# Expert steps of a mixture-of-experts block: activations laid out as 128 and twice 48 rows, five down products, transposes ahead of the down products

## The chip, the cores and the metric

The kernel runs on one NeuronCore of a Trainium2 chip. The metric is the time of one launch in device microseconds (us). The engines are PE (TensorE; PEld are its weight loads), DVE (VectorE), ACT (ScalarE), POOL (GpSimd) and SP (SyncE); each works through its own list of instructions in order and waits on semaphores.

## What is computed

One transformer block on 2048 rows of 256 numbers: a windowed attention, then a router that picks 4 of 16 experts for each row, the experts, and one shared expert for all rows. The change lies in the experts alone:

```python
w, idx = _router(xf, rg_w, ru_w, extra_scale, extra_bias)      # top 4 of 16
coeff = jnp.einsum('tk,tke->te', w, one_hot(idx, 16))
def step(y, ew):
    wg, wu, wd, c = ew                                         # 176x256, 176x256, 256x176
    h = jax.nn.silu(xf @ wg.T) * (xf @ wu.T)                   # 176 activations a row
    return (y + h @ wd.T * c[:, None], None)
y, _ = lax.scan(step, zeros, (Wg, Wu, Wd, coeff.T))
z = jax.nn.silu(xf @ Sg.T) * (xf @ Su.T) @ Sd.T                # the shared expert, 352 activations
x = x + gb * (y + z)
```

## The kernel before

Every fp32 product is made of three products of a reduced type: both factors are split into a high part (a copy to that type) and a low part (what is left), and high x high, low x high and high x low are summed in PSUM (`three`, L101).

The rows are sorted by expert through a scratch in HBM. Then come `NS` = 79 **expert steps** of 128 rows each (numbered 0 to 78), every one with the expert that a table names, so that the weights are addressed through a register; after them 16 **shared steps** (n = 0 to 15) of 128 rows for the shared expert. Both are software-pipelined over four lists. In step s:

- PE: `gate_up(s)`, six products into `GU`; `transpose_x(s+2)`, two transposes into `XT`; `down(s-2)`, six products into `YP`; `transpose_a(s-1)`, two transposes of the activations into `HT`. The 176 activations are taken as two blocks of 88 rows (`FH` = 88), so that down has two blocks of three products.
- ACT: `gate(s)` (silu), `x_hi(s+2)`, `a_hi(s-1)` (the high part of the transposed activations), and two small copies (`pick`).
- DVE: `gating(s)` (the activations `h_act`), `x_lo(s+2)`, `y_gate(s-2)` (the result times its coefficient), `a_lo(s-1)` (the low part). Eleven of steps 0 to 13 also carry `gu_low`, the low part of one expert's gate and up weights (704 columns); the last four steps carry four such pieces for the shared expert.
- POOL: it scatters the results of s to HBM by an indirect DMA, and in steps 0 to 7 makes `dn_low`, the low part of one expert's down weights. SP loads the 128 rows of step s+4.

The semaphores that matter: `down(w)` waits for `aT_lo` of w, `transpose_a(w)` for `gated` of w, `gate_up(w)` for `xT_lo2` of w, `y_gate(w)` for `y_mm` of w. `h_act`, `HT`, `aT`, `XT`, `GU` and `YP` have two buffers each. A shared step has twelve gate and up products, three transposes of 128 columns and nine down products; `add_late(n)` on DVE adds its result to the output.

## Time and profile before

| what | value |
|---|---|
| time, median of 3 runs | 569.58 us (567.87 to 569.83) |
| the profiled execution: its span, first to last instruction | 566.3 us |
| expert steps: first products of step 0 to those of shared step 0 | 321.2 to 502.2 us of the span |
| one expert step, steps 18 to 74 | 2.21 us |
| PE busy over the span | 87% |

The span is what the trace shows; a run's time has some 3.3 us more around it (569.58 less 566.3). Time stamps below are from the span's start. A group of instructions that overlap in their pipeline has a longer busy time than the distance between their starts, so that the distance is what counts for an engine that is full.

### The profile page before, as it was taken

Reading aid. Unit: us, or ns where it says so; the run is one execution under the profiler, and the core shown is the slowest. Engines: PE = TensorE matmul, PEld = TensorE weight load, DVE = VectorE, ACT = ScalarE, POOL = GpSimd, SP = SyncE. Lnnn points to the kernel's source line nnn. Section 1 sums busy time; section 2 is a strip of 40 time slices with the busy share of each in tenths; the row PEclk is TensorE's granted clock in tenths of the full one; section 3 lists DMA queues with packets and bytes.
Section 4 is the critical chain, followed back from the end, with each engine's and each line's share of the span. In section 5 each row is a group of like instructions: output and inputs, shape, how many; then the busy total and the mean of one; then the engine's idle time right before and its main releaser. Section 6 shows DMA issues by size and latency. Waiting matters only on the chain. (4 is left out here: it accounts for less than half of the span.)

```text
span 566.3 us, 12354 instructions
## 1 busy us (share of the span) xinstructions
PE 492.5 (87%) x3575; PEld 464.1 (82%) x3575; DVE 396.3 (70%) x1099; ACT 284.1 (50%) x743; POOL 291.9 (52%) x330
## 2 busy tenths in 40 slices
PE   2699999999999999998430488999999999999996
PEld 0589998999999898988330377999999999999995
DVE  6769953456867768687763798867777776784575
ACT  2368754554554545533262564555655655553331
POOL 6446603010346446465766799544444444446994
PEclk9999999999999999999555599999999999999999
DMA  7457996779747456422858443343434444356951
GB/s 196 134 170 217 254 307 205 196 206 229 209 125 216 139 164 183 124 86 83 267 203 271 135 132 103 116 136 119 140 120 127 132 124 137 119 158 249 413 204 74
DMA packets 62982, 98.00 MB, mean 173 GB/s; under 512 B 9747, under 2 KB 48210, under 8 KB 61574
## 3 DMA queue, kind: packets, MB, share of 16 engines
q1 hardware_dynamic: 50664, 57.80, 37.8%
q0 software_dynamic: 9136, 32.53, 15.2%
q10 hardware_dynamic: 3118, 6.89, 3.9%
q8 instruction: 31, 0.51, 0.4%
q14 instruction: 33, 0.27, 0.2%
HBM read 60.49 MB, written 40.04 MB: 178 GB/s over the span
## 5 line engine op out<-in xcount | busy, mean ns | idle before, releaser
L1702 POOL DMA_INDIRECT ys_scr<-h,ids_st x59 | 61.0, 1033 | 67.4 <-DVE h L1756 63.9
L140 POOL DMA_INDIRECT xs_scr<-h,slot_u x64 | 62.9, 982 | 54.0 <-PE TB L1302 26.6
L105 PE MATMUL GU<-gu_hi,xT 128*128 x316 | 84.1, 348 | 1.9 <-DVE xT L1736 1.9
L1626 ACT ACTIVATE aT<-HT 88x256 fp32r<-88x256 f32 (+1 forms) x95 | 37.8, 399 | 65.9 <-PE HT L1862 65.9
L105 PE MATMUL YP<-dn_hi,aT 88*128 x316 | 67.1, 304 | 4.4 <-DVE aT L1741 3.9
L1748 DVE TENSOR_TENSOR h_act<-GU,g_act 128x176 f32<-128x176 f32 (+1 forms) x95 | 35.2, 371 | 46.4 <-ACT g_act L1619 46.2
L919 ACT ACTIVATE prob<-TB 128x512 f32<-128x512 f32 x64 | 38.2, 597 | 56.5 <-PE TB L1302 55.8
L1312 PE MATMUL O<-raw,prob 128*128 128x99 f32 x512 | 66.2, 275 | 0.0
L1312 PEld LDWEIGHTS O<-raw,prob 128*128 128x128 f32 x512 | 61.6, 192 | 0.1
L105 PEld LDWEIGHTS YP<-dn_hi,aT 88*128 88x128 f32 x316 | 47.5, 188 | 11.1 <-issue 7.5
L105 PEld LDWEIGHTS GU<-gu_hi,xT 128*128 128x128 f32 x316 | 52.1, 192 | 2.3 <-issue 2.3
L1619 ACT ACTIVATE g_act<-GU 128x176 f32<-128x176 f32 (+1 forms) x95 | 32.4, 341 | 42.2 <-PE GU L105 42.0
L1741 DVE TENSOR_TENSOR aT<-HT,aT 88x256 fp32r<-88x256 f32 (+1 forms) x95 | 42.0, 442 | 15.4 <-ACT aT L1626 5.8
L105 PE MATMUL GU<-lo,xT 128*128 x158 | 51.7, 327 | 0.0
L1852 PE MATMUL XT<-ident,x_st 128*128 128x128 f32 x190 | 37.2, 278 | 15.3 <-DMA x_st<-xs_scr 15.2
L1044 DVE TENSOR_REDUCE neg_m<-SB 128x4 f32<-128x512 f32 x64 | 41.8, 686 | 6.4 <-PE SB L1290 6.0
L105 PE MATMUL YP<-lo,aT 88*128 x158 | 44.2, 280 | 0.0
L1852 PEld LDWEIGHTS XT<-ident,x_st 128*128 128x128 f32 x190 | 26.7, 143 | 18.8 <-DMA x_st<-xs_scr 16.1
L1736 DVE TENSOR_TENSOR xT<-XT,xT 128x256 fp32r<-128x256 f32 x95 | 39.9, 421 | 0.4 <-ACT xT L1613 0.3
L1290 PEld LDWEIGHTS SB<-dn_hi,gu_hi 97*128 97x128 f32 x240 | 36.2, 191 | 2.7
L1302 PEld LDWEIGHTS TB<-gu_hi,dn_hi 97*128 97x128 f32 x240 | 36.2, 191 | 2.7
L1862 PE MATMUL HT<-ident,h_act 128*88 128x128 f32 (+1 forms) x206 | 37.9, 272 | 0.0
(243 smaller groups left out, 1252.8 us busy)
## 6 DMA issues: line engine op xcount, KB each, us to landing
x_st<-xs_scr SPq DMA_DIRECT2D x79, 144.0 KB
dn_hi<-k_scr SPq DMA_DIRECT2D x48, 192.0 KB, 3.8
planes<-ys_scr POOLq DMA_DIRECT2D x8, 1024.0 KB, 17.1
k_scr<-raw SPq DMA_DIRECT2D x8, 768.0 KB, 6.1
dn_hi<-q_scr SPq DMA_DIRECT2D x24, 256.0 KB, 4.4
q_scr<-raw SPq DMA_DIRECT2D x8, 512.0 KB, 3.6
raw<-in_egu SPq DMA_DIRECT2D x8, 352.0 KB
raw<-in_x SPq DMA_DIRECT2D x16, 128.0 KB, 4.0
```

Source lines behind the costliest of these rows:

```text
L105: mm = eng.matmul(out, a, b, start=(i + j == 0), stop=(i == len(pairs) - 1 and j == 2))
L140: eng.indirect_dma_start(T["xs_scr"], bass.IndirectOffsetOnAxis(ap=T["slot_u"][:, par, t % 2, k:k + 1], axis=0), T["h2"][:, row, :], None) ...
L919: eng.activation(prob[:, q, :], TB[q % 2][:, :], ACT.Exp, scale=SCALE).then_inc(exp_done, 1)
L1044: eng.tensor_reduce(neg_m[:, p2, 4 * q:4 * q + 4], SB[q % 2][:, :].rearrange("p (h x) -> p h x", h=4), AX.X, ALU.max, negate=True).then_in ...
L1290: mm = eng.matmul(bank[:, hh * P:(hh + 1) * P], queries(n, t, 4 * q + hh), keys(par, 4 * q + hh, j), start=False, stop=True, skip_group_ch ...
L1312: mm = eng.matmul(O[:, head // 8, at:at + WIDE * VC], prob[:, q, hh * P:(hh + 1) * P], VW[:, bass.ds(HEADS * n + head, WIDE), :].rearrange ...
L1626: eng.activation(aT[0:rows, p2, 0, 0:k, :], HT[p2][0:rows, 0:k * P].rearrange("p (k x) -> p k x", k=k), ACT.Copy).then_inc(aT_hi, 1)
L1702: eng.indirect_dma_start(ys, bass.IndirectOffsetOnAxis(ap=ids_st[:, r:r + 1].bitcast(U32), axis=0), results(r % 8), None).then_inc(sent[q] ...
L1736: eng.tensor_tensor(xT[:, p2, 1, :, :], XT[p2][:, 0:D].rearrange("p (k x) -> p k x", k=KD), xT[:, p2, 0, :, :].bitcast(F32), ALU.subtract) ...
L1741: eng.tensor_tensor(aT[0:rows, p2, 1, 0:k, :], HT[p2][0:rows, 0:k * P].rearrange("p (k x) -> p k x", k=k), aT[0:rows, p2, 0, 0:k, :].bitca ...
L1852: mm = eng.transpose(XT[t % 2][:, k * P:(k + 1) * P], x_st[:, t, k * P:(k + 1) * P], ident[:, :])
L1862: mm = eng.transpose(HT[p2][0:rows, k * P:(k + 1) * P], h_act[:, p2, k * rows:(k + 1) * rows], ident[:, :])
```

## The change

The 176 activations are no longer cut in the middle. The first 128 make one block. The other 48 (`REST`) stand twice in the second block, at rows 0 to 47 and 64 to 111 (`SLOT` = 64), the rows between being zero: DVE writes them twice (one multiplication of 48 columns more), and after the transposes takes the high part off the second copy in place, so that one operand holds the high part above and the low part below. The second block of the down weights holds its 48 rows twice in the same places (the host lays them out so, with zeros between), and the block then needs two products (with the weights' high and low part) in place of three. `down` has five products. The low part of the activations is made by two instructions (64 rows x 128, 128 rows x 128) in place of one (88 rows x 256). Loads, high parts and low parts of the down weights have 128 rows in place of 88, and the memset of `h_act` 416 columns in place of 64.

The order moves too: on PE `transpose_a(s-1)` stands ahead of `down(s-2)`, on DVE `a_lo(s-1)` ahead of `y_gate(s-2)`, in the shared steps likewise, and after the last step the last but one down products stand ahead of the last transposes.

```diff
@@ gating, a_lo and step on DVE @@
+            if width == FI:
+                eng.tensor_tensor(h_act[:, p2, P + SLOT:P + SLOT + REST], up[:, P:FI], g_act[:, p2, P:FI], ALU.mult)
             eng.tensor_tensor(h_act[:, p2, 0:width], up, g_act[:, p2, 0:width], ALU.mult).then_inc(gated, 1)
-            eng.tensor_tensor(aT[0:rows, p2, 1, 0:k, :], HT[p2][0:rows, 0:k * P].rearrange("p (k x) -> p k x", k=k),
-                              aT[0:rows, p2, 0, 0:k, :].bitcast(F32), ALU.subtract).then_inc(aT_lo, 1)
+            eng.tensor_tensor(aT[SLOT:P, p2, 0, 1, :], HT[p2][SLOT:P, P:2 * P], aT[SLOT:P, p2, 0, 1, :].bitcast(F32),
+                              ALU.subtract)
+            eng.tensor_tensor(aT[:, p2, 1, 0, :], HT[p2][:, 0:P], aT[:, p2, 0, 0, :].bitcast(F32), ALU.subtract).then_inc(aT_lo, 1)
...
             x_lo(s + 2, p2)
+            if runs(s, 1):
+                a_lo(s - 1, 1 - p2)
             if runs(s, 2):
                 y_gate(s - 2, (r - 2) % UNROLL, i if r % 4 >= 2 else i - 1)
-            if runs(s, 1):
-                a_lo(s - 1, 1 - p2, FH, 2)
@@ down and step on PE @@
-            three(eng, YP[p2][:, 0:D],
-                  [(aT[0:FH, p2, 0, k, :], aT[0:FH, p2, 1, k, :], dn_of(dn_hi, e, k), dn_of(lo, e, k))
-                   for k in range(2)]).then_inc(y_mm, 1)
+            high, low, rest = aT[:, p2, 0, 0, :], aT[:, p2, 1, 0, :], aT[:, p2, 0, 1, :]
+            pairs = ((rest, dn_of(dn_hi, e, 1)), (rest, dn_of(lo, e, 1)), (high, dn_of(dn_hi, e, 0)),
+                     (low, dn_of(dn_hi, e, 0)), (high, dn_of(lo, e, 0)))
+            for i, (a, b) in enumerate(pairs):
+                mm = eng.matmul(YP[p2][:, 0:D], a, b, start=(i == 0), stop=(i == len(pairs) - 1))
+            mm.then_inc(y_mm, 1)
...
+            if runs(s, 1):
+                transpose_a(w - 1, 1 - p2)
             if isinstance(s, int) and 2 <= s < NE + 2:
                 eng.wait_ge(dn_lo, s - 1)
             if runs(s, 2):
                 down(w - 2, p2, before)
-            if runs(s, 1):
-                transpose_a(w - 1, 1 - p2, FH, 2)
@@ after the last shared step on PE @@
-        transpose_a(NS + TILES - 1, p2, P, SH_K)
-        for w in (NS + TILES - 2, NS + TILES - 1):
-            shared_down(w, w % 2)
+        shared_down(NS + TILES - 2, 1 - p2)
+        transpose_shared(NS + TILES - 1, p2)
+        shared_down(NS + TILES - 1, p2)
```

PE's list in an expert step before, from the load of the expert's number on (ISA sets up the register for the weights' address; the digit after `XT`, `YP`, `HT`, `GU` is the buffer):

```order
582 L1529 TENSOR_LOAD step_i
583 L1852 MATMUL XT0<-ident,x_st 128x128 x2
584 L105 ISA
585 L105 MATMUL YP0<-dn_hi,aT 128x256 x2
586 L105 ISA
587 L105 MATMUL YP0<-lo,aT 128x256
588 L105 ISA
589 L105 MATMUL YP0<-dn_hi,aT 128x256 x2
590 L105 ISA
591 L105 MATMUL YP0<-lo,aT 128x256
592 L1862 MATMUL HT1<-ident,h_act 88x128 x2
593 L105 ISA
```

The same place now:

```order
567 L1529 TENSOR_LOAD step_i
568 L1861 MATMUL XT1<-ident,x_st 128x128 x2
569 L1871 MATMUL HT0<-ident,h_act 128x128
570 L1872 MATMUL HT0<-ident,h_act 128x128
571 L1911 ISA
572 L1911 MATMUL YP1<-dn_hi,aT 128x256
573 L1911 ISA
574 L1911 MATMUL YP1<-lo,aT 128x256
575 L1911 ISA
576 L1911 MATMUL YP1<-dn_hi,aT 128x256 x2
577 L1911 ISA
578 L1911 MATMUL YP1<-lo,aT 128x256
```

The two transposes of the activations have moved from behind the down products to ahead of them, and of six down products five are left.

DVE's list in one of the first expert steps before, a step with a `gu_low` (the row `lo<-raw,gu_hi`); `h2<-YP` is a `y_gate`:

```order
639 L1748 TENSOR_TENSOR h_act<-GU1,g_act 128x176
640 L1736 TENSOR_TENSOR xT<-XT1,xT 128x256
641 L1756 SCALAR_TENSOR_TENSOR h2<-YP1,coef,gb 128x256
642 L1741 TENSOR_TENSOR aT<-HT0,aT 88x256
643 L1788 TENSOR_TENSOR lo<-raw,gu_hi 128x704
```

The same place now:

```order
648 L1756 TENSOR_TENSOR h_act<-GU1,g_act 128x48
649 L1757 TENSOR_TENSOR h_act<-GU1,g_act 128x176
650 L1736 TENSOR_TENSOR xT<-XT1,xT 128x256
651 L1742 TENSOR_TENSOR aT<-HT0,aT 64x128
652 L1744 TENSOR_TENSOR aT<-HT0,aT 128x128
653 L1765 SCALAR_TENSOR_TENSOR h2<-YP1,coef,gb 128x256
654 L1797 TENSOR_TENSOR lo<-raw,gu_hi 128x704
```

Two instructions came to DVE's step, and the low part of the activations moved ahead of the result.

## Rows read from the trace of the kernel before

**Rows 1.** Chain that ended last, steps 36 and 37: start us, us, engine, tile, line, count.

```profile
402.05 0.79 PE YP L105 x6
402.84 0.22 PE HT L1862 x2
403.06 0.97 PE GU L105 x6
404.03 0.22 PE XT L1852 x2
```

**Rows 2.** Busy time by stretch; PEclk is the granted clock.

```profile
326.00:358.00 32.00, 27.64 (x189) 24.85 (x188) 28.84 (x58) 17.60 (x65) 28.80 (x22) 1.00 0.40 113
...
367.50:493.30 125.80, 125.69 (x914) 120.61 (x913) 89.50 (x229) 74.02 (x285) 54.78 (x58) 1.00 0.41 128
493.30:502.20 8.90, 8.90 (x67) 8.52 (x65) 8.12 (x20) 6.58 (x21) 4.47 (x5) 1.00 0.37 120
```

**Rows 3.** Timeline of ACT in the same steps: start, us, [idle before <-releaser].

```profile
403.10 0.38 ACT L1626 ACTIVATE aT<-HT 88x256 fp32r<-88x256 f32 x1 [0.63 <-PE HT L1862]
```

**Rows 4.** Timeline of DVE in the same steps.

```profile
402.21 0.34 DVE L1748 TENSOR_TENSOR h_act<-GU,g_act 128x176 f32<-128x176 f32 x1 [0.48 <-ACT g_act L1619]
...
403.51 0.42 DVE L1741 TENSOR_TENSOR aT<-HT,aT 88x256 fp32r<-88x256 f32 x1
```

**Rows 5.** Timeline of PE in the same steps.

```profile
404.07 0.49 PE L105 MATMUL YP<-dn_hi,aT 88*128 x2
```

**Rows 6.** The chain again: the first shared step and a later one.

```profile
504.61 0.69 PE YP L105 x6
...
511.34 1.03 PE YP L105 x9
512.37 0.33 PE HT L1862 x3
```

**Rows 7.** Timeline of PE where steps 14, 18 and 75 begin.

```profile
358.29 0.57 PE L105 MATMUL GU<-gu_hi,xT 128*128 x2
...
367.58 0.56 PE L105 MATMUL GU<-gu_hi,xT 128*128 x2
...
493.35 0.57 PE L105 MATMUL GU<-gu_hi,xT 128*128 x2
```

**Rows 8.** Timeline of DVE in the first expert steps.

```profile
338.18 1.69 DVE L1788 TENSOR_TENSOR lo<-raw,gu_hi 128x704 fp32r<-128x704 f32 x1
339.79 0.33 DVE L1748 TENSOR_TENSOR h_act<-GU,g_act 128x176 f32<-128x176 f32 x1
340.04 0.41 DVE L1736 TENSOR_TENSOR xT<-XT,xT 128x256 fp32r<-128x256 f32 x1
340.37 0.47 DVE L1756 SCALAR_TENSOR_TENSOR h<-YP,coef,gb 128x256 f32<-128x256 f32 x1
340.76 0.41 DVE L1741 TENSOR_TENSOR aT<-HT,aT 88x256 fp32r<-88x256 f32 x1
341.10 0.32 DVE L1748 TENSOR_TENSOR h_act<-GU,g_act 128x176 f32<-128x176 f32 x1
...
342.43 0.48 DVE L1756 SCALAR_TENSOR_TENSOR h<-YP,coef,gb 128x256 f32<-128x256 f32 x1 [0.67 <-PE YP L105]
```

**Rows 9.** Groups of instructions by form: count | busy us, mean ns.

```profile
L1681 POOL TENSOR_TENSOR lo<-raw,dn_hi 88x512 fp32r<-88x512 f32 x16 | 23.7, 1495 | 6.5 <-POOLq L1992 6.3
...
L1729 POOL TENSOR_TENSOR planes<-planes 128x512 f32<-128x512 f32 x12 | 15.5, 1293 | 1.8 <-DMA to_add<-x_scr 1.8
```

**Rows 10.** The chain at the end of the program.

```profile
558.07 0.50 ACT aT L1626
...
559.21 1.30 PE YP L105 x9
...
560.88 0.56 DVE aT L1741
...
561.48 1.34 PE YP L105 x9
```

More of the change, by code:

```diff
@@ L20 @@
 NE, TOPK, FI = 16, 4, 176
-FH = FI // 2
+REST, SLOT = FI - P, P // 2
 SH_I = 2 * FI
@@ L174, in split_hi @@
     eng.activation(T["gu_hi"][:, e, :], T["raw"][:, e, 0:W_GU], ACT.Copy).then_inc(T["w_hi2"], 1)
-    eng.activation(T["dn_hi"][0:FH, e, :], T["raw"][0:FH, e, W_GU:W_EXP], ACT.Copy).then_inc(T["w_hi2"], 1)
+    eng.activation(T["dn_hi"][:, e, :], T["raw"][:, e, W_GU:W_EXP], ACT.Copy).then_inc(T["w_hi2"], 1)
 def fill_up(nc, eng, A, T, low, high):
@@ L1619, in gate, with a_hi @@
             eng.activation(g_act[:, p2, 0:width], bank[:, 0:width], ACT.Silu).then_inc(silu, 1)
-        def a_hi(w, p2, rows, k):
+        def a_hi(w, p2, k):
             eng.wait_ge(ht_mm, w + 1)
@@ L1625, in a_hi @@
                 eng.wait_ge(y_mm, w - 1)
-            eng.activation(aT[0:rows, p2, 0, 0:k, :], HT[p2][0:rows, 0:k * P].rearrange("p (k x) -> p k x", k=k),
+            eng.activation(aT[:, p2, 0, 0:k, :], HT[p2][:, 0:k * P].rearrange("p (k x) -> p k x", k=k),
                            ACT.Copy).then_inc(aT_hi, 1)
@@ L1671, in _ @@
             if n == 0:
-                a_hi(NS - 1, 1 - p2, FH, 2)
+                a_hi(NS - 1, 1 - p2, 2)
             else:
-                a_hi(NS + n - 1, 1 - p2, P, SH_K)
-        a_hi(NS + TILES - 1, (NS + TILES - 1) % 2, P, SH_K)
+                a_hi(NS + n - 1, 1 - p2, SH_K)
+        a_hi(NS + TILES - 1, (NS + TILES - 1) % 2, SH_K)
     @block.gpsimd
@@ L1788, in gu_low @@
             eng.tensor_tensor(lo[:, e, 0:W_GU], raw[:, e, 0:W_GU], gu_hi[:, e, :].bitcast(F32), ALU.subtract).then_inc(gu_lo, 1)
-        eng.memset(h_act[:, :, SH_I:SH_K * P], 0.0).then_inc(h_zero, 1)
+        eng.memset(h_act[:, :, FI:SH_K * P], 0.0).then_inc(h_zero, 1)
         for e in range(3):
@@ L1827, in _ @@
                 x_lo(NS + n + 2, p2)
+            if n == 0:
+                a_lo(NS - 1, 1 - p2)
+            else:
+                shared_lo(NS + n - 1, 1 - p2)
             if n < 2:
@@ L1834, in _ @@
                 add_late(n - 2)
-            if n == 0:
-                a_lo(NS - 1, 1 - p2, FH, 2)
-            else:
-                a_lo(NS + n - 1, 1 - p2, P, SH_K)
             for g in range(KEPT // 2):
@@ L1856, in x_pairs, with transpose_a, transpose_shared @@
             return xT[:, p2, 0, k, :], xT[:, p2, 1, k, :]
-        def transpose_a(w, p2, rows, blocks):
+        def transpose_a(w, p2):
             eng.wait_ge(gated, w + 1)
-            for k in range(blocks):
-                mm = eng.transpose(HT[p2][0:rows, k * P:(k + 1) * P], h_act[:, p2, k * rows:(k + 1) * rows], ident[:, :])
+            eng.transpose(HT[p2][:, 0:P], h_act[:, p2, 0:P], ident[:, :])
+            eng.transpose(HT[p2][:, P:2 * P], h_act[:, p2, P:2 * P], ident[:, :]).then_inc(ht_mm, 1)
+        def transpose_shared(w, p2):
+            eng.wait_ge(gated, w + 1)
+            for k in range(SH_K):
+                mm = eng.transpose(HT[p2][:, k * P:(k + 1) * P], h_act[:, p2, k * P:(k + 1) * P], ident[:, :])
             mm.then_inc(ht_mm, 1)
@@ L1929, in _ @@
                 transpose_x(w + 2, (w + 2) % 4, (w + 2) // 4 + 1)
+            if n == 0:
+                transpose_a(w - 1, 1 - p2)
+            else:
+                transpose_shared(w - 1, 1 - p2)
             if n < 2:
@@ L1933, in _ @@
                 shared_down(w - 2, p2)
-            if n == 0:
-                transpose_a(w - 1, 1 - p2, FH, 2)
-            else:
-                transpose_a(w - 1, 1 - p2, P, SH_K)
-        transpose_a(NS + TILES - 1, p2, P, SH_K)
-        for w in (NS + TILES - 2, NS + TILES - 1):
-            shared_down(w, w % 2)
+        shared_down(NS + TILES - 2, 1 - p2)
+        transpose_shared(NS + TILES - 1, p2)
+        shared_down(NS + TILES - 1, p2)
 def program(nc, A, out):
@@ L2057, in by_dim, with down_rows @@
         return np.asarray(w).reshape(2, HEADS // 2, DH, D).transpose(0, 2, 1, 3).reshape(D, D)
+    def down_rows(w):
+        rows = np.zeros((P, NE, 2, D), np.float32)
+        t = np.asarray(w).transpose(2, 0, 1)
+        rows[:, :, 0] = t[:P]
+        for first in (0, SLOT):
+            rows[first:first + REST, :, 1] = t[P:]
+        return rows
     g = {k.replace("L0_ffn_", "").replace("L0_attn_", "").replace("L0_", ""): np.asarray(v) for k, v in x.items()}
```

22 lines of the change are left out of this document (13 added, 9 removed).

## Prediction

> **What bounds the kernel now.** I read the chain that ended last first, for the expert steps hold 181 of the 566 us of the span. In a plain step (most of steps 14 to 74) it never leaves PE: six down products 0.79 us, two transposes of activations 0.22, six gate and up products 0.97, two transposes of rows 0.22, together 2.20 [rows 1]. The busy table by stretch says the same: over steps 18 to 74 PE is busy 125.69 of 125.80 us at the full granted clock, DVE 89.50 and POOL 54.78 [rows 2]. So a product taken off PE should show in the time. The second thing to see is that PE's "busy" hides a wait. Six expert down products take 0.79 us in a plain step, but 0.69 in the first shared step [rows 1, 6], where twelve gate and up products stand ahead of them and their operand is long ready. In the plain step the timelines show why: the transposes of the activations end at 403.06 [rows 1], ACT makes the high part from 403.10 to 403.48 [rows 3], DVE the low part from 403.51 to 403.93, and the first down product starts at 404.07 [rows 4, 5]. PE has finished the work in between by about then and waits some 0.10 us; the products in flight keep it counted as busy. That is a loop of four engines, and it sets the step, not PE's work alone.
>
> The opening is another regime. From 326 to 358 us, steps 2 to 13, DVE is busy 28.84 of 32.00 us and PE only 27.64 [rows 2]. The timeline shows DVE's rows without a gap, step after step, wherever a gu_low stands in them [rows 8].
>
> **The change part by part.**
>
> Sixth product. Nine shared down products, 128 rows deep, take 1.03 us, 0.114 each; the six of 88 rows took 0.69, 0.115 each [rows 6]. So the depth costs nothing, and one product less is 0.115 us a step.
>
> Transposes of 128 columns in place of 88: three take 0.33 in a shared step, two of 88 took 0.22 [rows 6, 1]: 0.11 each either way, nothing.
>
> The order on PE. Low parts of s-1 are now needed a whole step later, behind gate_up, four transposes and the down products of s-2. The 0.10 us goes. What is late next? transpose_a(s-1) now stands ahead of down(s-2), and its wait for gating holds those down products, and through them y_gate and POOL's scatter. In the trace gating runs from 402.21 to 402.55 [rows 4]; its gate and up products ended one step before those that end at 404.03 [rows 1], at 401.83, so it is done 0.72 us after them. With the new instruction ahead of it, that is some 0.85. The transposes want it 0.22 + 0.22 + 0.58 + 0.97 + 0.22 = 2.2 us after that point. Cover 1.35 us: nothing in a plain step.
>
> A plain step is then 0.97 + 0.22 + 0.22 + 5 x 0.115 = 1.98 us against 2.20, a gain of 0.22 (0.115 for the product, 0.105 for the wait). DVE must follow in 1.98. Its chain, from start to start where it is full, is 0.25 (h_act), 0.33 (xT), 0.39 (result), 0.34 (aT), 1.31 together [rows 8].
>
> What the change adds on DVE. From 176 to 256 columns the distance grows by 0.08, so 0.001 a column and 0.07 for an instruction: 48 columns take 0.12, and 128 columns 0.20, two of them 0.40 in place of 0.34. The low bound is 0.19 a step. The high bound takes every instruction's full busy time instead (0.33, 0.41 and so on [rows 8], less the columns): 0.20 + 2 x 0.28 - 0.34 = 0.42, and a little for the overlap that the neighbours lose: 0.45. No row that I read has a DVE instruction on rows 64 to 127 among others that begin at row 0, so neither end is shown. I take 0.32, the middle. The step's chain is then 1.63, at most 1.76, and ends inside 1.98: nothing in a plain step.
>
> One rule of the Trainium skill speaks to this (VectorE: DVE Perf Modes, section "Two Vector instructions with no wait between them"): a Vector instruction that begins in another group of 32 partitions than the one before it in the same memory is held until all earlier ones have finished. By it the piece on rows 64 to 127 and the one behind it both wait, the overlap of 0.08 is lost twice, the addition is 0.35, and the sum below would end at 557.8; without it, at the low bound, at 555.8. No row here shows it.
>
> The opening, steps 0 to 13. Twelve full steps at 0.32 on an engine without gaps are 3.8 us, steps 0 and 1 some 0.3, the wider memset, 352 columns more at 0.001, at most 0.35, taken as 0.3. Against it stand DVE's 3.16 us of idle time in that stretch [rows 2]: its gaps are waits for down products that wait for DVE, as the 0.67 ahead of the result at 342.43 [rows 8], a turn of the loop that the new order opens. I let 2.0 of it go; the rest waits for ACT's high parts of weights. Opening: +2.4 (from 12 x 0.19 + 0.5 - 3.0 = -0.2 to 12 x 0.45 + 0.7 - 1 = +5.1).
>
> Wider down weights. POOL's low parts are 512 columns of 88 rows, 1495 ns as a mean beside a busy DVE; its sums of 512 columns and 128 rows take 1293 [rows 9]. Rows cost nothing there, nor on ACT. The loads grow by 40 rows of 2 KB an expert, 1.3 MB in all, most of it before the experts begin; the DMA engines are busy 0.4 of the time in the expert steps [rows 2]. I count nothing.
>
> Steps 14 to 17 take 367.58 - 358.29 = 9.29 us [rows 7] and become 4 x 1.98 = 7.92: -1.4. Steps 18 to 74 are 57 in 493.35 - 367.58 = 125.77 [rows 7]: 57 x 0.22 = 12.5 off. In the last four, DVE is busy 8.12 of 8.90 us [rows 2] with the shared expert's low parts, and 4 x 0.32 is more than its 0.78 idle: DVE wants 9.4, PE may run the 1.35 us of cover ahead of it, and I count nothing (-0.9 to +0.5). The first two shared steps lose one product each, -0.2; the other shared steps hold no such wait and stay.
>
> The end. The last but one down products wait for their low part until 559.21 and run 1.30; the last low part cannot start before 560.88, behind the sum of those products on DVE; the last products run 1.34 from 561.48 [rows 10]. In the new order the last but one low part is made during the nine products ahead (1.03 [rows 6]), so these products start about 1.0 us sooner; behind them come the last transposes (0.33 [rows 6]), ACT (0.50) and DVE (0.56) [rows 10], with the hand-overs 1.5 in place of the 0.97 from 560.51 to 561.48: 0.5 back. Net -0.5.
>
> Sum: +2.4 - 1.4 - 12.5 + 0 - 0.2 - 0.5 = -12.2. The profiled span of 566.3 becomes 554.1; with the 3.3 us that lie around it, the median of 569.6 becomes **557.4**.
>
> **Rivals.**
>
> DVE sets the plain step. If nothing on it overlaps, its step is 0.20 + 0.34 + 0.42 + 0.28 + 0.28 + 0.48 = 2.0 to 2.05 us and the gain 0.16: 57 x 0.16 = 9.1, the opening +5.1, the end steps +0.5: 569.6 + 5.1 - 0.9 - 9.1 + 0.5 - 0.7 = 564.5. For it: the new instruction on rows 64 and up, unseen so far. Against it: its rows do overlap in every full stretch [rows 8].
>
> The 0.10 us stays, because it is PE's own cost of turning from transposes to products whose weights are addressed by register, not the wait. Then 61 steps gain 0.115: 557.4 + 6.4 = 563.8. Against it: the first shared step turns in the same way and shows 0.69 [rows 6].
>
> The change does not do what it says, since something else paces a step at 2.2 us (the setting of registers, the row loads, POOL): only the opening's cost is left, 569.6 + 2.4 - 0.7 = 571.3, no change. Against it: POOL and DMA have half of the step free [rows 2].
>
> Slower. DVE's chain becomes serial with PE's. The place is each plain step: if the idle 0.48 ahead of h_act [rows 4] stays in the chain, and every instruction counts in full, a step is 2.05 + 0.48 + 0.1 = 2.6, 0.42 over the present one: 57 x 0.42 = 24, the opening +5: about 598. It decides from 2.21 us a step on, 0.9 of added work. Against it: no wait of PE closes that loop, since h_act of step s is wanted only in step s+1.
>
> **How the numbers follow.** Forecast 0.71, DVE paces 0.12, the wait stays 0.08, nothing moves 0.05, slower 0.04. The forecast's own range goes from 554.5 (opening -0.2) to 561 (opening +5.1). Runs of this kernel differ by 0.35%, so that 0.5%, 2.8 us, is about what can be told from no change. All but the last two cases are faster by more; I leave 0.02 more for a mishap within the bound. Range 553.8 to 564.8: it takes in the first three cases and leaves some 0.13 out, theirs and the last two.
>
> **What would show it.** In the trace after: a plain step of 1.98 us from gate and up to gate and up; five down products in 0.58 of the chain; the low part ready more than a microsecond before them; DVE's chain at 1.5 to 1.75 where it is full, and whether the piece on rows 64 to 127 starts only when the one before it has ended; the opening to step 14 longer or shorter than now by at most 3 us. A plain step of 2.05 with DVE without gaps is the first rival, 0.69 for five products the second, 2.2 the third. I am wrong if the steps gain less than 0.15, or if the opening costs more than 5 us.

## The result and the profile after

The changed kernel takes 561.14 us (median of six runs, 559.41 to 562.00) against 569.21 of the kernel before in the same job: a ratio of 0.985, 95% interval 0.981 to 0.988. The forecast was 557.4, the range 553.8 to 564.8: the direction and the range were right, the size was 3.7 us too good. The profiled run took 562.0, with a span of 560.1 in place of 566.3. Ratios leave out the runs that fell in a slower state of the chip, among them one of the order alone (568.18).

The page after: the first line is busy time and share by engine, the second the shares of the chain that ended last.

```profile
PE 480.7 (86%) x3496; PEld 454.3 (81%) x3496; DVE 414.3 (74%) x1257; ACT 274.6 (49%) x743; POOL 288.1 (51%) x330
...
PE 26%; DVE 8%; DMA 5%; issue 2%; POOL 1%; ACT 1%; ACTq 0%; DVEq 0%; POOLq 0%
```

PE has 79 products less, one for each expert step. DVE has 158 instructions more, and it now has 8% of the chain, the DMA 5%.

The busy windows after, to be read beside [rows 2]: stretch and length, then PE, PEld, DVE, ACT, POOL, granted clock, DMA share, GB/s. They are steps 2 to 13, 14 to 17, 18 to 74 and 75 to 78.

```profile
328.10:362.10 34.00, 27.58 (x183) 24.36 (x181) 33.47 (x83) 17.60 (x70) 27.83 (x23) 1.00 0.36 113
362.10:370.70 8.60, 8.40 (x60) 8.07 (x61) 7.96 (x27) 4.31 (x18) 3.61 (x4) 1.00 0.47 128
370.70:485.10 114.40, 114.20 (x857) 112.06 (x856) 100.49 (x343) 67.78 (x286) 54.68 (x57) 1.00 0.47 141
485.10:494.80 9.70, 8.72 (x62) 7.98 (x61) 9.36 (x29) 6.42 (x22) 4.33 (x5) 1.00 0.45 142
```

Steps 18 to 74 fell from 125.8 to 114.4 us, PE still full. In steps 2 to 13 DVE is now busy 33.47 of 34.00, and in steps 75 to 78 9.36 of 9.70 while PE has a whole microsecond free: DVE sets the time there, though in steps 2 to 13 a part of its busy time is a wait for POOL, as the experiments show.

A plain step in the chain after (start us, us, engine, tile, line, count), beside [rows 1]:

```profile
402.04 0.22 PE XT L1861 x2
402.26 0.11 PE HT L1871
402.37 0.11 PE HT L1872
402.48 0.59 PE YP L1911 x5
403.07 0.96 PE GU L105 x6
404.04 0.22 PE XT L1861 x2
```

From transposes to transposes this is 2.00 us; the average of the undisturbed steps is 1.986, against 1.98 forecast and 2.20 before. DVE's low part and the down products that want it, from the timelines of the same steps:

```profile
403.55 0.29 DVE L1744 TENSOR_TENSOR aT<-HT,aT 128x128 fp32r<-128x128 f32 x1
404.23 0.36 PE L1911 MATMUL YP<-dn_hi,aT 128*128 x1
```

The low part is ready at 403.84, 0.39 us ahead of the products. The prediction looked for more than a microsecond there.

The next table has the durations of the stages in every kernel of this study, each the distance between two starts in PE's timeline: "first" is the start of the first expert product (in us of the span), "14-17" the time from the first product of step 14 to that of step 18 and so on; "shared 2-14" goes to the start of the last shared step, "end" from there to the end of the last sum on DVE, and "store" is what follows it in the span.

| kernel | first | 0-13 | 14-17 | 18-74 | 75-78 | shared 0-1 | shared 2-14 | end | store |
|---|---|---|---|---|---|---|---|---|---|
| before | 321.2 | 37.05 | 9.29 | 125.77 | 8.89 | 6.72 | 45.52 | 8.78 | 3.0 |
| after | 323.9 | 38.14 | 8.65 | 114.41 | 9.68 | 6.73 | 46.58 | 8.33 | 3.7 |
| after, again (e11) | 321.9 | 38.13 | 8.66 | 114.43 | 9.69 | 6.72 | 46.59 | 8.33 | 3.4 |
| order alone (e1) | 325.2 | 33.50 | 8.45 | 120.37 | 8.44 | 6.67 | 46.36 | 8.33 | 5.3 |
| five products alone (e2) | 320.7 | 38.25 | 10.01 | 131.52 | 9.95 | 6.73 | 45.83 | 8.78 | 2.4 |
| before, wide loads (e5) | 320.3 | 36.93 | 9.20 | 125.74 | 8.88 | 6.74 | 45.97 | 8.79 | 2.4 |
| no hold, by a mask (e3) | 322.2 | 36.31 | 8.43 | 113.88 | 9.16 | 6.74 | 46.58 | 8.34 | 3.7 |
| no hold, rows 0 to 63 (e9) | 322.8 | 36.06 | 8.36 | 113.67 | 8.97 | 6.74 | 46.83 | 8.33 | 3.4 |
| one low part (e7) | 322.6 | 36.05 | 8.28 | 113.83 | 8.83 | 6.74 | 46.67 | 8.34 | 3.4 |
| entries loaded once (e6) | 320.9 | 38.15 | 8.61 | 113.25 | 9.69 | 6.73 | 46.67 | 8.33 | 3.4 |
| sums a step later (e4) | 323.5 | 38.16 | 8.68 | 114.41 | 9.68 | 6.72 | 46.94 | 8.32 | 3.8 |
| e7 + e6 + e4 (e8) | 322.5 | 36.18 | 8.31 | 113.22 | 8.82 | 6.73 | 46.72 | 8.37 | 3.8 |
| e7 + e6, sums spread (e10) | 322.1 | 36.41 | 8.29 | 113.23 | 8.83 | 6.73 | 46.66 | 8.36 | 3.8 |
| e7 + e6, pair sooner (e12) | 321.5 | 36.03 | 8.27 | 113.25 | 8.83 | 6.73 | 45.64 | 8.33 | 5.1 |

The stages repeat within 0.05 us from one trace of the changed kernel to the next. The first and the last column don't: they hold the attention and the landing of the last store. So stages are compared with stages below, and whole times only with their scatter in mind. The ratios are each to the kernel before in the same job; between jobs that kernel's own median goes from 569.2 to 570.8.

### The profile page after: what moved, and what is told of

The parts are those of the page before. It is cut to its first block and busy times, and to the rows that moved or that the text cites. A ratio compares the mean times of both kernels' runs of the same rounds, so it can differ in the third digit from the quotient of the medians.

```text
span 560.1 us, 12354 instructions
## 1 busy us (share of the span) xinstructions
PE 480.7 (86%) x3496; PEld 454.3 (81%) x3496; DVE 414.3 (74%) x1257; ACT 274.6 (49%) x743; POOL 288.1 (51%) x330
## 5 line engine op out<-in xcount | busy, mean ns | idle before, releaser
L1702 POOL DMA_INDIRECT ys_scr<-h,ids_st x59 | 58.4, 990 | 63.2 <-DVE h L1765 61.4
L105 PE MATMUL GU<-gu_hi,xT 128*128 x316 | 78.3, 330 | 2.5 <-DVE xT L1736 1.9
L1911 PE MATMUL YP<-dn_hi,aT 128*128 x237 | 57.0, 309 | 5.8 <-DVE aT L1744 5.6
L1911 PEld LDWEIGHTS YP<-dn_hi,aT 128*128 128x128 f32 x237 | 39.0, 188 | 8.2 <-issue 8.1
L1911 PE MATMUL YP<-lo,aT 128*128 x158 | 44.2, 280 | 0.0
L1626 ACT ACTIVATE aT<-HT 128x256 fp32r<-128x256 f32 (+1 forms) x95 | 38.0, 400 | 3.3 <-PE HT L1878 2.4
L1613 ACT ACTIVATE xT<-XT 128x256 fp32r<-128x256 f32 x95 | 36.4, 383 | 1.6 <-PE XT L1861 1.5
L105 PE MATMUL QB<-gu_hi 128*128 128x256 f32 (+1 forms) x192 | 32.3, 329 | 2.9 <-DVE gu_hi L544 2.9
```

Source lines behind the costliest of these rows:

```text
L105: mm = eng.matmul(out, a, b, start=(i + j == 0), stop=(i == len(pairs) - 1 and j == 2))
L1613: eng.activation(xT[:, p2, 0, :, :], XT[p2][:, 0:D].rearrange("p (k x) -> p k x", k=KD), ACT.Copy).then_inc(xT_hi2, 1)
L1626: eng.activation(aT[:, p2, 0, 0:k, :], HT[p2][:, 0:k * P].rearrange("p (k x) -> p k x", k=k), ACT.Copy).then_inc(aT_hi, 1)
L1702: eng.indirect_dma_start(ys, bass.IndirectOffsetOnAxis(ap=ids_st[:, r:r + 1].bitcast(U32), axis=0), results(r % 8), None).then_inc(sent[q] ...
L1911: mm = eng.matmul(YP[p2][:, 0:D], a, b, start=(i == 0), stop=(i == len(pairs) - 1))
```

## The experiments

**The order alone and the five products alone.** The change has two halves, and each was put alone into the kernel before. The order alone, on PE (on DVE `a_lo` likewise ahead of `y_gate`, and the shared steps and the tail as in the change):

```diff
             transpose_x(w + 2, (t + 2) % 4, i + (2 if t >= 2 else 1))
+            if runs(s, 1):
+                transpose_a(w - 1, 1 - p2, FH, 2)
 ...
                 down(w - 2, p2, before)
-            if runs(s, 1):
-                transpose_a(w - 1, 1 - p2, FH, 2)
```

> The kernel before with the new order alone (transposes of s-1 ahead of the down products of s-2, low part ahead of the result, the shared steps and the tail likewise); two blocks of 88 rows and six products stay. Theory, a loop of four engines (transposes, ACT's high part, DVE's low part, down products) holds each plain step by 0.105 us: a plain step falls from 2.20 to 2.09 or 2.10, six down products take 0.69 in the chain in place of 0.79, 61 steps give -6.4 and the end -0.45: 562.0 to 563.0 against 569.2. Rival, the 0.10 is PE's own cost of turning to products with weights addressed by register: a step stays at 2.20 and the time is 568.5 to 569.0.

Measured: 564.96 us (four runs, 557.73 to 568.18) where 562.0 to 563.0 was expected, ratio 0.987 [0.979, 0.995]; the profiled run starts its experts late, at 325.2, and ends with a store of 5.3, so its time is longer than expected while its stages are not. They are shorter, by 9.9 in all where 6.9 was expected, for the opening gains 3.6 as well. A plain step takes 2.11. Its chain:

```profile
402.26 0.22 PE HT L1862 x2
402.48 0.71 PE YP L105 x6
403.19 0.97 PE GU L105 x6
```

The six down products take 0.71 in place of the 0.79 of [rows 1]: some 0.09 of the 2.20 was the wait, as forecast (0.105). The rival, that turning to weights addressed by register costs it, falls.

The five products alone: the changed kernel, its order put back on PE (shown), on DVE, in the shared steps and in the tail.

```diff
-            if runs(s, 1):
-                transpose_a(w - 1, 1 - p2)
             if isinstance(s, int) and 2 <= s < NE + 2:
                 eng.wait_ge(dn_lo, s - 1)
             if runs(s, 2):
                 down(w - 2, p2, before)
+            if runs(s, 1):
+                transpose_a(w - 1, 1 - p2)
```

> The changed kernel (128 and twice 48 rows, five products, all its DVE work) in the old order: down products of s-2 ahead of the transposes of s-1, result ahead of the low part. Theory of the loop: from the end of the transposes to the first down product the loop takes 2.20 - 0.69 - 0.22 = 1.29 us in the kernel before, and DVE's low part in two instructions adds 0.1 to 0.18, so that a plain step is 1.39 to 1.47 + 0.57 + 0.22 = 2.18 to 2.26, no gain at all from the product that is gone; with the opening's extra work the time is 568 to 573. Rival, PE's own work sets the step: 2.20 - 0.115 = 2.085, time 562.5 to 564.

Measured: 578.21 us where 568 to 573 was expected, ratio 1.017 [1.012, 1.022]; a plain step takes 2.29, longer than with six products. Its chain, and DVE's timeline in the same step (start us, us, engine, line):

```profile
402.46 0.22 PE XT L1861 x2
402.68 0.03 issue
402.70 0.91 PE YP L1911 x5
403.61 0.11 PE HT L1871
```

```profile
401.32 0.48 DVE L1765 SCALAR_TENSOR_TENSOR h<-YP,coef,gb 128x256 f32<-128x256 f32 x1
401.95 0.29 DVE L1742 TENSOR_TENSOR aT<-HT,aT 64x128 fp32r<-64x128 f32 x1
402.26 0.29 DVE L1744 TENSOR_TENSOR aT<-HT,aT 128x128 fp32r<-128x128 f32 x1
```

Five products stand in the chain with 0.91 us, where the changed kernel has 0.59. The low part that DVE began at 402.26 ends at 402.55, the first product starts at 402.70, and the 0.03 of issue ahead of it shows that PE has nothing left in flight: the piece holds the wait and the refilling of PE's pipeline, some 0.3 a step, as much as the plain steps differ by (2.29 and 1.986). So the loop of transposes, high part, low part and down products sets the step, a little later still than the 2.18 to 2.26 expected, and the two-piece low part made it longer by more than the product that was taken away: the low part lasts 0.60 us there (401.95 to 402.55) and 0.42 in the kernel before [rows 4], while the product was worth 0.115. So the halves don't add: over steps 18 to 74 the order alone gives 5.4 us, the five products alone cost 5.8, and both together give 11.4. The five products are worth something only once the loop is open.

**What DVE pays for the second copy.** DVE's timeline of the changed kernel where it is full, beside [rows 8]: start us, us, line, form.

```profile
357.17 0.41 DVE L1736 TENSOR_TENSOR xT<-XT,xT 128x256 fp32r<-128x256 f32 x1
357.62 0.29 DVE L1742 TENSOR_TENSOR aT<-HT,aT 64x128 fp32r<-64x128 f32 x1
357.93 0.29 DVE L1744 TENSOR_TENSOR aT<-HT,aT 128x128 fp32r<-128x128 f32 x1
358.13 0.47 DVE L1765 SCALAR_TENSOR_TENSOR y_st<-YP,coef,gb 128x256 f32<-128x256 f32 x1
358.53 0.88 DVE L1797 TENSOR_TENSOR lo<-raw,gu_hi 128x704 fp32r<-128x704 f32 x1
```

In [rows 8] each instruction begins before the one ahead of it has ended. Here the piece on rows 64 to 127 begins 0.03 after the end of `xT`, and the piece behind it 0.01 to 0.02 after its end; from there on they overlap again. Two kernels take the other start row away. The first makes the same difference on all 128 rows, with a column `lower` of 0 and -1:

```diff
-            eng.tensor_tensor(aT[SLOT:P, p2, 0, 1, :], HT[p2][SLOT:P, P:2 * P], aT[SLOT:P, p2, 0, 1, :].bitcast(F32),
-                              ALU.subtract)
+            eng.scalar_tensor_tensor(out=aT[:, p2, 0, 1, :], in0=aT[:, p2, 0, 1, :].bitcast(F32), scalar=lower[:, 0:1],
+                                     in1=HT[p2][:, P:2 * P], op0=ALU.mult, op1=ALU.add)
```

> The changed kernel, but the low part of the second copy is taken off by one instruction on all 128 rows (high part times a column of 0 and -1, plus the transposed value, stored rounded) in place of the one on rows 64 to 127, so that every DVE instruction of a step begins at row 0; as many columns and as many instructions as in the changed kernel. Theory, DVE holds an instruction that begins in other rows until the earlier ones have ended: xT to the piece falls from 0.44 to about 0.33, the piece to the next from 0.31 to about 0.21, the step's chain from 1.71 to 1.50; the opening, steps 13 to 15 and the last four steps lose 2 to 3 us together, time 558 to 559.5 against 561.1 of the changed kernel, plain steps stay at 1.98. Rival, the gaps of 31 and 13 ns belong to the small size or to what the pieces read: chain 1.70, time 560.5 to 561.5.

Measured: 557.09 us, ratio to before 0.981 [0.976, 0.985]. DVE's timeline in it, where the piece now begins 0.33 after `xT`:

```profile
356.36 0.41 DVE L1737 TENSOR_TENSOR xT<-XT,xT 128x256 fp32r<-128x256 f32 x1
356.69 0.33 DVE L1743 SCALAR_TENSOR_TENSOR aT<-aT,lower,HT 128x128 fp32r<-128x128 f32 x1
356.94 0.28 DVE L1745 TENSOR_TENSOR aT<-HT,aT 128x128 fp32r<-128x128 f32 x1
```

The hold is gone. But this kernel changes the number of rows together with the first row, so the second leaves the size alone and moves the instruction to the first copy, which has the same weights:

```diff
-            eng.tensor_tensor(aT[SLOT:P, p2, 0, 1, :], HT[p2][SLOT:P, P:2 * P], aT[SLOT:P, p2, 0, 1, :].bitcast(F32),
+            eng.tensor_tensor(aT[0:SLOT, p2, 0, 1, :], HT[p2][0:SLOT, P:2 * P], aT[0:SLOT, p2, 0, 1, :].bitcast(F32),
                               ALU.subtract)
```

> The changed kernel, but the high part is taken off the first copy (rows 0 to 63) in place of the second (rows 64 to 127); both copies have the same weights, so the result is the same. One slice changes: the instruction has the same size and begins at row 0. Theory, what holds DVE is that the instruction begins in other rows than those around it: xT to the piece falls from 0.44 to 0.33, the piece to the next from 0.31 to 0.21, the chain from 1.71 to 1.50, time 556.5 to 558.5. Rival, what holds it is that it has 64 rows beside neighbours of 128: the gaps of 31 and 13 ns stay, the chain stays at 1.71, time 560.5 to 561.5.

Measured: 557.31 us (554.67 to 557.65), ratio to before 0.973 [0.967, 0.979]; the changed kernel took 559.75 in the same job. DVE's timeline in it:

```profile
358.97 0.40 DVE L1736 TENSOR_TENSOR xT<-XT,xT 128x256 fp32r<-128x256 f32 x1
359.30 0.27 DVE L1742 TENSOR_TENSOR aT<-HT,aT 64x128 fp32r<-64x128 f32 x1
359.50 0.27 DVE L1744 TENSOR_TENSOR aT<-HT,aT 128x128 fp32r<-128x128 f32 x1
359.69 0.46 DVE L1765 SCALAR_TENSOR_TENSOR h<-YP,coef,gb 128x256 f32<-128x256 f32 x1
```

The same 64 x 128 piece overlaps on both sides: 0.33 and 0.20 from start to start in place of 0.45 and 0.31. The first row is what holds it, and the hold costs 0.23 us a step on a full DVE. By stages it is worth 2.1 us in steps 0 to 13, 0.3 in 14 to 17, 0.7 in 18 to 74 and 0.7 in 75 to 78, 3.8 together. The medians differ by 2.4 in the same job (559.75 and 557.31) and by 3.8 from the first job's 561.14, with starts and stores that scatter by as much. The rule that the prediction weighed, of the Trainium skill (VectorE: DVE Perf Modes, section "Two Vector instructions with no wait between them"), that an instruction starting in another group of 32 partitions is held until all earlier ones have finished, is what these traces show, for the piece and for the one behind it.

The third kernel drops an instruction. ACT makes the high part in two pieces, 128 x 128 and rows 64 to 127 of the second block, whose other rows are zero; DVE makes the low and the mixed block at once, and the products read the mixed block from there (DVE's part shown):

```diff
-            eng.tensor_tensor(aT[SLOT:P, p2, 0, 1, :], HT[p2][SLOT:P, P:2 * P], aT[SLOT:P, p2, 0, 1, :].bitcast(F32),
-                              ALU.subtract)
-            eng.tensor_tensor(aT[:, p2, 1, 0, :], HT[p2][:, 0:P], aT[:, p2, 0, 0, :].bitcast(F32), ALU.subtract).then_inc(aT_lo, 1)
+            eng.tensor_tensor(aT[:, p2, 1, 0:2, :], HT[p2][:, 0:2 * P].rearrange("p (k x) -> p k x", k=2),
+                              aT[:, p2, 0, 0:2, :].bitcast(F32), ALU.subtract).then_inc(aT_lo, 1)
```

> The changed kernel, but ACT makes the high part in two pieces (128 x 128, and rows 64 to 127 of the second block, whose rows 0 to 63 are set to zero once), and DVE then makes the low part of the first block and the mixed second block by a single instruction of 128 rows x 256 columns, stored rounded. DVE has one instruction less a step and none that begins at row 64. Theory, DVE's chain goes from 1.71 to 0.12 + 0.25 + 0.33 + 0.34 + 0.39 = 1.43: the opening and steps 13 to 17 lose 2.5 to 3.5 us, the last four steps up to 1, plain steps stay at 1.98 to 1.99; time 557 to 558.5. Rival, ACT's second instruction (0.2 to 0.3 a step, beside the high parts of weights it makes in steps 0 to 2) makes ACT the engine that the opening waits for: time 560 to 562.

Measured: 556.12 us (555.28 to 556.96) where 557 to 558.5 was expected, ratio to before 0.975 [0.971, 0.979]. The low part in DVE's timeline, and what follows it:

```profile
356.92 0.42 DVE L1746 TENSOR_TENSOR aT<-HT,aT 128x256 fp32r<-128x256 f32 x1
357.26 0.48 DVE L1768 SCALAR_TENSOR_TENSOR h<-YP,coef,gb 128x256 f32<-128x256 f32 x1
```

One instruction of 256 columns takes 0.34 to the next start, the two unheld ones 0.40. Against the kernel without the hold the stages hardly move any more (steps 0 to 13 36.05 and 36.06). The rival does not come: ACT's second instruction did not make the opening longer, though DVE waits for ACT's silu twice in it, 1.3 us together.

**What DVE's busy time in the opening holds.** In steps 4 to 10 POOL makes its low parts of the down weights (`dn_low`) beside DVE's `gu_low`. POOL in the kernel before, beside the `gu_low` of [rows 8] that runs from 338.18 to 339.87:

```profile
337.82 1.29 POOL L1681 TENSOR_TENSOR lo<-raw,dn_hi 88x512 fp32r<-88x512 f32 x1
339.28 1.44 POOL L1702 DMA_INDIRECT ys_scr<-h,ids_st  x1 [0.17 <-issue]
```

POOL and DVE in the same step of the changed kernel:

```profile
341.77 1.27 POOL L1681 TENSOR_TENSOR lo<-raw,dn_hi 128x512 fp32r<-128x512 f32 x1
342.53 1.28 DVE L1797 TENSOR_TENSOR lo<-raw,gu_hi 128x704 fp32r<-128x704 f32 x1
```

In both kernels each `gu_low` of these steps ends 0.76 us after the `dn_low` beside it, whenever it began, and takes 1.3 to 2.4 us; where POOL makes none it takes 0.88 (the one at 358.53 above). So a part of DVE's busy time is a wait for POOL, whose list waits for no other engine there in the kernel before. Where DVE comes to its `gu_low` later, the wait is shorter: steps 6, 7, 10 and 11 take 2.9 to 3.0 us in both kernels, though DVE's other instructions take 0.40 more. Steps 0 to 5 take 16.3 in place of 15.2, steps 6 to 13 21.8 in both. No run takes POOL's work away, so how much of the opening is POOL's is not shown.

**The steps that are longer than 1.98.** Steps 23 and 24, 47 and 48, 71 and 72 of the changed kernel take 2.21 and 2.17. PE starts its table of entries over every 24 steps, with three loads in its list. One kernel keeps all entries:

```diff
-            if first:
-                entry.clear()
-                entry[0] = load_entry(s)
-            k = len(entry) - 1
-            gate_up(w, p2, entry[k])
+            if s == 0:
+                entry[0] = load_entry(0)
+            gate_up(w, p2, entry[s])
 ...
-            if not last:
-                entry[k + 1] = load_entry(s + 1)
+            if s < NS - 1:
+                entry[s + 1] = load_entry(s + 1)
```

> The changed kernel, but PE keeps the table's entries in registers over the whole program and loads each entry once, in place of starting over every 24 steps with three loads. Theory, the reloads on PE's sequencer hold the products at steps 23/24, 47/48 and 71/72, which take 2.21 + 2.16 in place of 2 x 1.98: these pairs fall to 3.96 to 4.0, steps 18 to 74 from 114.4 to 113.2, time 559.9. Rival, the three pairs are long for something else that comes every 24 steps (instruction fetch, the result's wait): they stay at 4.2 to 4.4.

Measured: 557.99 us where 559.9 was expected, steps 18 to 74 113.25 in place of 114.41: 1.16 of the 1.2 expected. PE's timeline, the last down product and the first gate and up product behind it, where steps 23 and 24 of the changed kernel begin, then where step 24 begins with entries loaded once:

```profile
380.52 0.28 PE L1911 MATMUL YP<-lo,aT 128*128 x1
380.64 0.48 PE L105 MATMUL GU<-gu_hi,xT 128*128 x2
...
382.51 0.28 PE L1911 MATMUL YP<-lo,aT 128*128 x1
382.86 0.58 PE L105 MATMUL GU<-gu_hi,xT 128*128 x2
```

```profile
379.44 0.28 PE L1911 MATMUL YP<-lo,aT 128*128 x1
379.56 0.48 PE L105 MATMUL GU<-gu_hi,xT 128*128 x2
```

The first product of step 24 starts 0.35 after the down product ahead of it, in place of 0.12. With the order alone (steps of 2.11) these pairs are not longer than others; with the first copy (rows 0 to 63) the first step of a pair is short again (1.98) and the second takes 2.13 to 2.15. In the kernel before, steps 24, 48, 71 and 72 take 2.26, 2.29, 2.28 and 2.48, the three pairs together 0.5 more than plain steps. So the loads can be covered, and part of what they cost goes by way of DVE; what decides it was not tried. The median is 3.1 us below the changed kernel's first one, from another job; of that the stages hold 1.1, and the experts start at 320.9 in place of 323.9 (321.9 the second time), so the rest is not shown to be the edit's.

**The shared step that is longer.** Shared step n = 11 takes 4.41 in place of 3.53. The chain has the last load of results but one there, and DVE's timeline shows what waits for it:

```profile
511.83 23.64 DMA planes<-ys_scr
```

```profile
535.50 1.64 DVE L1786 TENSOR_TENSOR planes<-planes 128x1024 f32<-128x1024 f32 x1 [1.45 <-DMA planes<-ys_scr]
537.06 0.51 DVE L1757 TENSOR_TENSOR h_act<-GU,g_act 128x352 f32<-128x352 f32 x1
```

The sum waits 1.45 us for the landing, and the gating of the next step, which needs no load, stands behind it in DVE's list. In the kernel before that sum started without a wait. Three kernels move it. The sums a step later:

```diff
-    STORED = (2, 3, 4, 0, 5, 6, 1, 7)
-    ADDS = (10, 13)
+    STORED = (2, 3, 4, 5, 0, 6, 1, 7)
+    ADDS = (11, 13)
```

> The changed kernel with the sums of the first kept pair of output tiles one shared step later on DVE (n = 11 to 13 in place of 10 to 12; the stores' order follows). Theory, in the changed kernel DVE stands 1.4 us at that sum until the last loads of the results have landed, with the gating of the next shared step behind it, and shared step n = 11 takes 4.41 in place of 3.53: that step falls to 3.5 to 3.6 and the shared steps from n = 2 to 15 from 46.6 to 45.7, time 560.0 to 560.5 against 561.1. Rival, the loads then hold another sum or the last store, and the time stays at 561.

Measured: 562.00 us, stage 46.94. Step n = 11 is 3.49, but n = 14 takes 4.63, since two sums now stand together, and beside them a sum of POOL:

```profile
544.71 1.74 POOL L1729 TENSOR_TENSOR planes<-planes 128x512 f32<-128x512 f32 x1
544.13 1.17 DVE L1793 TENSOR_TENSOR to_add<-to_add,planes 128x512 f32<-128x512 f32 x1
545.22 2.31 DVE L1786 TENSOR_TENSOR planes<-planes 128x1024 f32<-128x1024 f32 x1
547.45 0.51 DVE L1757 TENSOR_TENSOR h_act<-GU,g_act 128x352 f32<-128x352 f32 x1
```

The time stays, as the rival said, but no row there waits for a load. The sum of 1024 columns takes 2.31 and ends 1.08 us after the sum of POOL that ran when it began, as it does in the changed kernel at n = 11 (1.64): DVE's sums too wait for POOL inside their busy time. The three edits so far together:

> The three preceding edits together (sums one step later, entries loaded once, low part in one instruction). If they act in different stretches their gains add: -0.9, -1.2 and -3 from 561.1 give 556.0, with 1 to either side. If one of them only moves the wait to the next, the time is that of the best of them alone.

Measured: 556.53 us. The gains of the low part and of the entries add by stages (36.18 and 113.22), that of the sums does not exist. Then the sums one by one over steps 11 to 15:

```diff
-            for g in range(KEPT // 2):
-                if ADDS[g] <= n < ADDS[g] + 3:
-                    add_kept(g, n - ADDS[g])
+            for g, part in {11: ((0, 0),), 12: ((0, 1), (0, 2)), 13: ((1, 0),), 14: ((1, 1),), 15: ((1, 2),)}.get(n, ()):
+                add_kept(g, part)
```

> Low part in one instruction, entries loaded once, and the six sums of the kept output tiles spread over the shared steps 11 to 15 (first pair: 11, 12, 12; second pair: 13, 14, 15), so that no step carries the last sum of one pair and the long first sum of the other, which in the run with both a step later stood together at n = 13 and made n = 14 take 4.63. Expected: no shared step over 3.75, shared steps n = 2 to 15 in 45.6 to 46.0 in place of 46.7, time 555.0 to 556.0 against 556.5 of the run with the three edits together. Rival, the long sum is slowed by POOL's sums beside it and one step alone can't hold it: n = 14 stays at 4 or more and the time at 556 to 556.5.

Measured: 556.03 us, stage 46.66 where 45.6 to 46.0 was expected; n = 13 takes 4.10 and n = 14 3.74. No gain either: the long sum of n = 14 takes 2.25 and again ends 1.08 after POOL's, so the rival's cause is seen, in two steps in place of one. Last, the load itself sooner, the sums where they were:

```diff
-    LOADED = (2, 3, 4, 5, 6, 7, 0, 1)
+    LOADED = (2, 3, 4, 5, 6, 0, 7, 1)
```

> Low part in one instruction, entries loaded once, and the results of the first kept pair of output tiles loaded as the sixth of eight in place of the seventh (the pair that POOL needs last takes the seventh place); the sums stand where they stand in the changed kernel. Theory, what holds gating in shared step n = 11 is the landing of that load alone, which comes 1.4 to 1.5 us after DVE is ready for it: one load sooner is about 2 us, n = 11 falls from 4.41 to 3.5 or 3.6, shared steps n = 2 to 15 from 46.6 to 45.7, time 555.0 to 555.5. Rival, as in the two runs that moved the sums, the lost time comes back in a later step (POOL's load is late, or DVE's sums beside POOL's): 46.6 stays and the time is 556.

Measured: 556.10 us (554.43 to 556.79) where 555.0 to 555.5 was expected, stage 45.64, n = 11 3.53. The sum starts without a wait:

```profile
527.03 1.22 DVE L1789 TENSOR_TENSOR planes<-planes 128x1024 f32<-128x1024 f32 x1
528.99 0.52 DVE L1760 TENSOR_TENSOR h_act<-GU,g_act 128x352 f32<-128x352 f32 x1 [0.74 <-ACT g_act L1619]
```

So the landing was the cause, and the 1.0 us is recovered in its stage. It came with the new order: the order alone has n = 11 at 4.20 with the same wait, the five products alone 3.62 without it. In the whole time it is not seen: in the profiled run the last store takes 1.3 us longer than in the run with the sums spread.

**The start.** The changed kernel's profile reaches the experts 2.7 us later than before. Ahead of them its loads differ, shown here for one of three places, the high parts of the down weights and the memset of `h_act` (0.41 us in place of 0.11).

```diff
 ...
-    eng.dma_start(T["raw"][0:FH, at, W_GU:W_EXP], A["ed"][:, at].rearrange("p e k x -> p e (k x)")).then_inc(loaded, 16)
+    eng.dma_start(T["raw"][:, at, W_GU:W_EXP], A["ed"][:, at].rearrange("p e k x -> p e (k x)")).then_inc(loaded, 16)
 ...
```

> The kernel before with nothing but wider loads: the down weights come from an array of 128 rows an expert (rows 88 to 127 zero and not used), 40 rows of 2 KB more for each of 16 experts. Theory, the wider loads cost the attention the 2.6 us by which the profiled run of the changed kernel enters the experts later (last table work at 304.97 in place of 302.36): time 571 to 572, the experts entered near 305. Rival, that difference is scatter from run to run: time 568.5 to 570, entry within 1.5 us of 302.4, and the entries of the other kernels here lie on both sides of it whatever their loads.

Measured: 567.46 us, ratio 0.996 [0.993, 1.000], the first expert product at 320.3, earlier than before. The wider loads cost nothing. The memset comes too late to be the cause: PE's last work for the table begins at 304.4 in place of 301.8, 13 us ahead of it. And the changed kernel once more:

> The changed kernel once more, for where it enters the experts. If the 2.6 us by which its first profile enters later than the kernel before is scatter from run to run, the entry lies anywhere between 301 and 306. If it belongs to this program, whatever its instructions there, the entry is again near 304.9 and the time 561; the step that takes a pair 23/24, 47/48 and 71/72 is again 2.21 + 2.16.

Measured: 559.75 us, the first expert product at 321.87 where its first profile has 323.92. The two rows, of the wide loads in the kernel before and of the changed kernel again (PE's timelines, with the idle time ahead and what ended it):

```profile
320.29 0.95 PE L105 MATMUL GU<-gu_hi,xT 128*128 x2 [1.78 <-DVE xT L1736]
```

```profile
321.87 0.66 PE L105 MATMUL GU<-gu_hi,xT 128*128 x1 [1.80 <-DVE xT L1736]
```

Over all fourteen traces that start lies between 320.3 and 325.2, whatever the loads. Most of the 2.7 is scatter. Whether a part of it belongs to a program, as some kernels' runs lie close together (entries loaded once: 557.5 to 558.2), the runs don't settle.

## Why the prediction was right, and where its sizes were off

The mechanism of the forecast held in the plain steps, and no rival came. The sum was -12.2; the stages from the first expert product to the last sum give 242.03 - 232.53 = 9.5 us. The terms that were too good are off by 4.0 together, and the opening, counted 1.3 too dear, hides a third of that; this was luck, for the opening's cost came elsewhere than counted. The median fell by 8.1, the profiled span by 6.2: it starts its experts 2.7 later and ends with 0.6 more. What lies around the span, 3.3 us in the prediction, is 1.9 in the changed kernel's profiled run. By its steps:

- **Sixth product, order, plain step.** Right. The wait was 0.09 (order alone) where 0.105 was forecast, the product 0.126 (2.112 to 1.986) where it was 0.115; the step 1.986 against 1.98. Transposes of 128 columns cost 0.11 each, as taken. The cover of 1.35 us for the new wait of `transpose_a` was enough; the low part's lead of 0.39 us is less than half of what the prediction looked for, but enough too. What was not said is that the halves need each other: the five products alone would have lost.
- **Steps 18 to 74.** -11.4 in place of -12.5. The missing step is the loading of entries every 24 steps, 1.16 by experiment. It was not in the sum at all. The same pairs are 0.5 longer than plain steps in the kernel before, so 0.7 of the miss is theirs; the other 0.4 is that a plain step gained 0.212, which was rounded to 0.22.
- **What DVE gains in work.** Mis-sized: 0.40 a step in place of 0.32, since a chain of 1.71 stands against 1.31. The low bound of 0.19 is what the same instructions cost without the hold (chain about 1.49). The hold was named, with its rule and the right place, and priced at twice the lost overlap of 0.08, 0.16; it costs 0.23, because the held instruction also starts 0.01 to 0.03 after the end of the one ahead. The middle was taken between two ends that were two cases, hold or none; one of them had to be chosen.
- **The opening.** +1.1 in place of +2.4. In steps 2 to 13 DVE's busy time went up by 4.0 (29.45 to 33.47 in windows cut at the steps), near the 3.8 counted, and of its idle time of 3.15 all but 0.53 went, 2.6 in place of the 2.0 allowed. The wider memset, counted at 0.3, stands ahead of the first product. What the prediction had wrong is the reading of [rows 8]: it took DVE's rows without a gap for work, and so put a cost on each of twelve steps. Steps 0 to 5 have all of the 1.1 and steps 6 to 13 none, and the `gu_low` in between hold a wait for POOL that a longer chain uses up. POOL's 28.80 us of 32.00 stood beside DVE's 28.84 in [rows 2] and was not weighed for the opening. With the order alone steps 0 to 13 fall by 3.6, 3.1 of it from step 6 on, where the `gu_low` at steps 8 and 9 find no `dn_low` running as they begin and take 0.88 in place of 1.85 and 1.70; the second copy takes 4.6 there.
- **Steps 14 to 17.** -0.6 in place of -1.4. DVE leaves step 13 behind, with a last `gu_low`, and steps 13 to 15 take 2.51, 2.51 and 2.15. The prediction let the plain step begin at once at step 14.
- **The last four steps.** +0.8 in place of 0, outside its bound of +0.5. The sentence "4 x 0.32 is more than its 0.78 idle" was right and said 9.4; the cover of 1.35 us that was to swallow the rest was not there, since the first shared products wait 0.64 us for the gating of step 78, which stands in DVE's list behind the shared expert's low parts. Without the hold the stage is 8.97, with one low part 8.83, shorter than before.
- **Shared steps.** 0 and +1.06 in place of -0.2 and 0. The first two are set by the loop of gate and up products, silu and gating (PE waits 0.18 us for it at 498.17), not by the down products that went. The rest is the landing of the results: counted from the first shared step their loads are issued at 12.3 us in place of 11.0, while DVE reaches the sum sooner, and it waits 1.45 us. "The other shared steps hold no such wait and stay" is the sentence that failed.
- **The end.** -0.45 against -0.5; the order alone has the whole of it.
- **Wider loads and weights.** Nothing, as counted.

With the low part in one instruction, the entries loaded once and the load sooner, more than the sum is recovered: 227.1 us from the first product to the last sum, 14.9 less than before. Several versions beat both kernels: one slice changed gives 557.3, one low part 556.1, ratios to before of 0.973 and 0.975, each in its own job. What is added to the latter (entries, load) shows in its stages but not in the whole time, which stays at 556.0 to 556.5.

A last reading of the table is a caution: from the first product to the last sum the order alone takes 232.1, the whole change 232.5. The five products and their second copy gave 6.0 us in steps 18 to 74 and took 4.6 in steps 0 to 13, 1.2 in 75 to 78 and 0.5 elsewhere. With the copy on the other rows they are worth 3.2.

## What to carry to other kernels

Before an instruction is taken off a full engine, look for a loop through other engines that its waits close: six products in 0.79 against 0.69 elsewhere showed one, and taking a product away without opening the loop made the step longer. Work that is moved to an engine with room on average is paid in the stretches where that engine is full, so price it there, instruction by instruction, from start to start, and look first whether busy time there is work: an instruction whose duration changes with what another engine runs beside it may be waiting. Let all Vector instructions of a tight chain begin at the same row: here one slice was worth 3.8 us in the stages.

## What the runs showed that was not expected

- A Vector instruction on rows 64 to 127 between others from row 0 starts 0.03 us after the end of the one ahead, and the next one 0.01 to 0.02 after its end; on rows 0 to 63 the same instruction starts 0.08 before that end (medians over 77 steps). The price is 0.11 us each.
- Three loads of table entries in PE's list cost nothing in a step of 2.11 us and some 0.4 in a pair of steps of 1.98.
- A subtraction of 704 columns on DVE ends 0.76 us after the one of 512 columns on POOL that runs beside it, and takes 0.88 us alone; a sum of 1024 columns on DVE ends 1.08 after POOL's. The wait shows as busy time.
- The time from the start of the program to the experts differs by 2.0 us between two traces of the same program, whose stages behind it repeat within 0.05; over all fourteen traces it differs by 4.9, and the time after the last sum by 2.9.
